# Windowed attention: the value projection in four pieces, one a round, with earlier output transposes and transposes of 113 rows

## The chip, the cores and the metric

The kernel runs on one core of one Trainium2 chip. The metric is the device time of one execution, in microseconds (us), the median of the runs of one kernel. A change of about 2% is what separates faster or slower from no change here.

## The reference, cut to what matters

`x` is (16, 64, 56, 56) in float32. Two attention layers follow each other, each on a group-normalised input and each with a residual. The change touches the first alone:

```python
t = xn.reshape(Bb, Cc, WS, n1, WS, n2).transpose(0, 3, 5, 2, 4, 1)
tok = t.reshape(Bb * n1 * n2, WS * WS, Cc)          # windows of 49 tokens
qk = (tok @ qk_w.T).reshape(-1, WS * WS, 2, HEADS, DH)
attn = softmax(einsum('bhqd,bhkd->bhqk', q, k) * scale)
v = relu(tok @ v_w.T)
o = einsum('bhqk,bhkd->bhqd', attn, v)
x = x + out                                          # residual
```

The reshapes take four windows together: 196 tokens of 64 channels become 49 rows of 16 heads of 16, so a softmax runs over 49 keys, for 256 groups of four windows. The second layer is a 5x5 local attention with a softmax over 25 neighbours; the change does not touch it.

## The kernel before, in words

Two images lie side by side on the 128 partitions (2 x 64 channels), 8 such pairs. A **unit** is one row of 8 windows (two groups of four) in both images of a pair, 392 columns on 128 partitions; there are 64 units. Units 0 to 6 are written out (PEEL), units 7 to 62 run in a loop of two units a turn, and unit 63 is written out again. Units 0 to 5 also carry the statistics of the later images on VectorE, and unit 6 turns them into scales.

Each unit has four **rounds**, k = 0 to 3. A round handles one image's group of four windows, with its 16 heads; its number over the whole stage is n = 4u + k. The steps are software-pipelined over rounds and units, and each engine runs its list in the order in which it is written; semaphores tie the lists together. In round k of unit u:

- TensorE: `scores(n)` into PSUM banks 2 and 3; `transpose_probs(n-1)` (four transposes into bank 7); `weigh_values(n-2)` (into bank 6); in rounds 1 and 2 one half of `project_qk` for unit u+1; then a wait until VectorE has taken this round's scores out of banks 2 and 3 (`sub_done`) and GpSimd has expanded the next keys (`kbd_ready`); then `transpose_v` in round 0, one half of `project_v` (bank 0, for unit u+1) in rounds 1 and 2, `transpose_output` of unit u-1 in round 3. `transpose_v` and `transpose_output` share bank 1.
- VectorE: `subtract_max(n)` (the maximum, then the subtraction), `normalise(n-2)`, and in round 3 `order_tokens(u-1)`, two copies out of bank 1 that put the result in token order; in round 1 the statistics of a finished unit.
- ScalarE: `copy_transposed(n-1)` out of bank 7, `exponentials(n)`, then `place_values` in rounds 0 and 1, `copy_qk` for unit u+1 in rounds 2 and 3, `gather(u+2)` in round 2 and `copy_v(u+1)` last in round 3. `copy_v` counts `proj_copied` up to 3(u+2).
- GpSimd: `expand_keys` for each round, and `add_residual(u-2)` in round 1. SyncE stores the finished units.

`await_project(u+1)` in TensorE's list waits for the tokens of unit u+1 and for `proj_copied` at 3(u+1), that is for `copy_v(u)`: banks 0, 4 and 5 are written again after it. It stands in round 1 before `transpose_probs`. `transpose_v(u)` waits for the same count. Each attention matrix has 49 real rows in a slot of 64, two slots in 128 rows: rows 113 to 127 are padding. The lines of the profile: `scores` L1312, `transpose_probs` L1321, `weigh_values` L1337, `project_qk` L1281, `project_v` L1289, `transpose_v` L1300, `transpose_output` L1351; VectorE L1100, L1104 (`subtract_max`), L1114, L1117 (`normalise`), L1129 (`order_tokens`); ScalarE L844 (`gather`), L850 (`copy_qk`), L854 (`copy_v`), L863 (`place_values`), L868 (`exponentials`), L875 (`copy_transposed`).

Of the kernel before, what the change touches and what calls it, by code (L numbers as in the profile page):

```python
# [21 lines left out]
P = 128  # L22
# [8 lines left out]
S = WS * WS  # L31
SP = 64
ELT = 4 * S
UT = 2 * ELT
HEADS_R = 8
HEADS_T = HEADS_R // 2
UNITS = BP * NI
# [7 lines left out]
STATS_UNIT = 6  # L45
# [255 lines left out]
def build(nc, x, bn_gamma, bn_beta, bn_mean, bn_var, qk_w, v_w, w_out, b_out, out):  # L301
# [11 lines left out]
    with ExitStack() as ctx:  # L313
# [20 lines left out]
        ident = const(P)  # L334
# [370 lines left out]
        def _(pool):  # L705
# [38 lines left out]
            for u in range(2):  # L744
                for b2 in range(2):
                    nc.gpsimd.memset(qk_sb[u][b2][:, UT:UT + SP], 0.0)
                    nc.gpsimd.memset(v_bd[u][b2], 0.0)
                nc.gpsimd.memset(v_ch[u], 0.0)
            nc.gpsimd.memset(zeros, 0.0).then_inc(zeros_ready, 1)
            for q in probs:  # L750
                i = nc.gpsimd.memset(q, 0.0)
# [76 lines left out]
        def _(act):  # L828
# [42 lines left out]
            def copy_transposed(n, k, ready=True):  # L871
                act.wait_ge(pt_done, n + 1)
                if not (isinstance(n, int) and n < 2):
                    act.wait_ge(pv_done, n - 1)
                nc.scalar.activation(probs_T[k % 2].rearrange("p j n -> p (j n)"), PS[:, 7, :],  # L875
                                     ACT.Copy).then_inc(pt_copied, 1)

            gather(0, 0)
# [146 lines left out]
        def _(dve):  # L1025
# [70 lines left out]
            def subtract_max(n, k):  # L1096
                b0, b1 = score_banks
                bank = PS[:, b0:b1 + 1, 0:HEADS_T * SP].rearrange("p i (j s) -> p i j s", s=SP)[:, :, :, 0:S]
                dve.wait_ge(s_done, n + 1)
                nc.vector.tensor_reduce(by_tile(row_max[k % 2]), bank, AX_X, ALU.max).then_inc(max_done, 1)  # L1100
                dve.wait_ge(max_done, n + 1)
                if not (isinstance(n, int) and n < 4):
                    dve.wait_ge(pt_done, n - 3)
                nc.vector.tensor_tensor(probs[k].rearrange("p (j i) s -> p i j s", i=2)[:, :, :, 0:S], bank,  # L1104
                                        by_tile(row_max[k % 2]).unsqueeze(3).to_broadcast([P, 2, HEADS_T, S]),
                                        ALU.subtract).then_inc(sub_done, 1)
# [24 lines left out]
            def unit(u, up, first, last):  # L1131
                for k in range(4):
                    n = 4 * u + k
                    subtract_max(n, k)
                    if not (first and k < 2):
                        normalise(n - 2, (k - 2) % 4, up if k >= 2 else 1 - up)
                    if isinstance(u, int) and u == STATS_UNIT and k >= 1:
                        i = group_stats(k - 1, 1, CHUNKS)
                        if k == 3:
                            affine(group_stats(3, 1, CHUNKS), PAIRS_OF_TURN[1])  # L1140
                    if k == 3 and not first:
                        order_tokens(u - 1, 1 - up)
                    if k == 1 and not (isinstance(u, int) and u < 4):
                        unit_stats(u - 4)
                    if isinstance(u, int) and u < STATS_UNIT:
                        step(stats(STATS_OF[n]))
# [105 lines left out]
        def _(pe):  # L1252
# [6 lines left out]
            def pair_means(turn, k):  # L1259

                pe.wait_ge(gn_in, 2 * turn + k + 1)
                nc.tensor.matmul(PS[:, 1, 0:BP], pair_mean, t_tmp, start=True, stop=True).then_inc(gn_out, 1)
# [20 lines left out]
                if h == 1:  # L1283
                    i.then_inc(qk_done, 1)

            def project_v(up, h):

                cols = slice(h * ELT, (h + 1) * ELT)
                i = nc.tensor.matmul(PS[:, 0, cols], wv_T, tok[up][:, cols], start=True, stop=True)  # L1289
                if h == 1:  # L1290
                    i.then_inc(v_done, 1)

            def transpose_v(u, up):
# [22 lines left out]
            def transpose_probs(n, k):  # L1316
                pe.wait_ge(exp_done, n + 1)
                if not (isinstance(n, int) and n < 1):
                    pe.wait_ge(pt_copied, n)
                for j in range(4):  # L1320
                    i = nc.tensor.transpose(PS[:, 7, j * P:(j + 1) * P],  # L1321
                                            probs[k][:, 2 * j:2 * j + 2, :].rearrange("p h s -> p (h s)"), ident)
                i.then_inc(pt_done, 1)

            def await_values(n, vbd):
# [15 lines left out]
            def await_output(u):  # L1341

                pe.wait_ge(norm_done, 4 * u + 4)
                pe.wait_ge(vbd_ready, 2 * UNITS if isinstance(u, int) and u == UNITS - 1 else 2 * u + 4)

            def transpose_output(up):

                for e in range(2):
                    for h in range(2):
                        q = 2 * e + h  # L1350
                        i = nc.tensor.transpose(PS[:, 1, q * P:(q + 1) * P], o_tok[up][:, e, h].rearrange("p b c -> p (b c)"), ident)  # L1351
                i.then_inc(ot_done, 1)

            await_project(0)
            for h in range(2):
                project_qk(0, h)
                project_v(0, h)

            def unit(u, up, first, last):
                for k in range(4):  # L1360
                    n = 4 * u + k
                    m = (k - 2) % 4
                    scores(n, k, up)
                    if not (first and k < 2):
                        await_values(n - 2, 2 * u + m % 2 + 1 - (0 if k >= 2 else 2))
                    if k == 1 and not last:
                        await_project(u + 1)
                    if not (first and k == 0):
                        transpose_probs(n - 1, (k - 1) % 4)
                    if not (first and k < 2):  # L1370
                        weigh_values(n - 2, m, up if k >= 2 else 1 - up)
                    if k in (1, 2) and not last:
                        project_qk(1 - up, k - 1)
                    if isinstance(u, int) and u == STATS_UNIT and k >= 2:
                        pe.wait_ge(vbd_ready, 2 * u + 2)
                        pair_means(1, k - 2)
                        if k == 3:
                            pe.wait_ge(sq_in, 2)
                    if k == 3 and not first:
                        await_output(u - 1)  # L1380
                    if not (last and k == 3):
                        pe.wait_ge(kbd_ready, n + 2)
                        pe.wait_ge(sub_done, n + 1)
                    if k == 0:
                        transpose_v(u, up)
                    elif k in (1, 2) and not last:
                        project_v(1 - up, k - 1)
                    elif k == 3 and not first:
                        transpose_output(1 - up)
            units(pe, unit, peel=PEEL)  # L1390
            transpose_probs(4 * UNITS - 1, 3)
            for k in (2, 3):
# [127 lines left out]
```

## Time and profile before

| what | value |
|---|---|
| median of 3 runs | 1789.05 us (1788.67 to 1808.39) |
| the profiled execution | 1798.7 us, span 1797.0 us |
| first attention | until about 770 us of the span |
| VectorE's share of the span | 80% |
| TensorE's share of the span | 80% |

The profile is of one execution. A row of its timeline gives the start and length of a group of equal instructions, both in us; TensorE matmuls are pipelined, so one's length reaches into the next, and what a step costs is read from its start to the start of the next step. "PEld" is the load of the stationary operand. A float32 matmul is listed as two instructions, a transpose as one. The value in brackets is the idle time ahead of the row and the instruction that ended it.

### The profile page before, as it was taken

The numbers are of one execution on the slowest core, as the hardware profiler recorded it, in microseconds if no ns is written. First come the engines' busy times: TensorE is split into PE (matmuls) and PEld (weight loads), VectorE is DVE, ScalarE is ACT, GpSimd is POOL, SyncE is SP. The second block draws the span as 40 slices with busy tenths as digits, with TensorE's granted clock in tenths as the row PEclk, the third lists the DMA queues.
The fourth block names the chain that finished last, engine by engine and source line by source line (L and its number), as shares of the span: only waits on it lengthen the run. The fifth ranks groups of instructions, "written<-read, shape, count | busy, mean of one in ns | idle before, by whom it ended". The sixth has DMA issues, their size and how long they took to land.

```text
span 1797.0 us, 60281 instructions
## 1 busy us (share of the span) xinstructions
PE 1435.7 (80%) x25001; PEld 704.2 (39%) x25001; DVE 1434.3 (80%) x1975; ACT 1051.5 (59%) x1883; POOL 1187.3 (66%) x860
## 2 busy tenths in 40 slices
PE   4999999999999999936887869777786876867745
PEld 2656666666666666610222212212221221213322
DVE  4776777777777777769999998999989899995924
ACT  3446777777777777735555747466574656543300
POOL 5334555555555555500999899999999999995700
PEclk9568999999999999956898998999999899997868
DMA  8702010202015101060225133252312422026079
GB/s 334 278 11 55 18 54 18 54 18 54 18 49 87 54 18 54 18 165 7 56 51 128 29 75 78 50 129 51 88 49 59 115 51 67 22 68 247 21 289 390
DMA packets 106860, 156.12 MB, mean 87 GB/s; under 512 B 71362, under 2 KB 83650, under 8 KB 100034
## 3 DMA queue, kind: packets, MB, share of 16 engines
q1 hardware_dynamic: 106690, 153.60, 29.2%
q8 instruction: 137, 2.24, 0.5%
q14 instruction: 33, 0.27, 0.1%
HBM read 81.92 MB, written 65.20 MB: 82 GB/s over the span
## 4 chain that ended last, share of the span: by engine, by line
PE 39%; POOL 27%; DVE 16%; issue 12%; ACT 2%; SPq 1%; DMA 1%; DVEq 0%; POOLq 0%
POOL arena L800 20%; PE PS L1312 6%; PE PS L1471 5%; PE PS L1321 5%; PE PS L1337 5%; POOL arena L811 4%; DVE arena L1104 4%; PE PS L1289 4%; DVE arena L1100 4%; PE PS L1281 4%; PE PS L1494 3%; PE PS L1300 2%; PE PS L1351 2%; DVE arena L1211 2%; PE PS L1419 2%
## 5 line engine op out<-in xcount | busy, mean ns | idle before, releaser
L800 POOL TENSOR_TENSOR arena<-arena 128x2016 f32<-128x2016 f32 (+2 forms) x168 | 604.9, 3635 | 78.9 <-PE PS L1419 78.7
L1211 DVE TENSOR_TENSOR arena<-arena,PS 128x1568 f32<-128x1568 f32 x348 | 610.3, 1778 | 39.6 <-PE PS L1471 32.6
L766 POOL TENSOR_TENSOR arena<-arena,consts 128x196 f32<-128x196 f32 x512 | 294.3, 608 | 278.1 <-ACT arena L850 278.1
L1471 PE MATMUL PS<-arena,consts 32*32 32x392 f32 x12800 | 391.3, 513 | 83.8 <-DVE arena L1211 46.9
L992 ACT ACTIVATE PS<-arena 128x392 f32<-128x392 f32 x348 | 172.9, 499 | 271.4 <-DVE arena L1211 269.5
L1419 PE MATMUL PS<-arena,consts 128*32 128x504 f32 (+2 forms) x1664 | 225.6, 618 | 119.9 <-POOL arena L800 76.7
L1471 PEld LDWEIGHTS PS<-arena,consts 32*32 32x32 f32 x12800 | 140.2, 104 | 337.4 <-DVE arena L1211 179.1
L1100 DVE TENSOR_REDUCE arena<-PS 128x8 f32<-128x392 f32 x256 | 143.3, 560 | 142.3 <-PE PS L1312 140.9
L875 ACT ACTIVATE arena<-PS 128x512 f32<-128x512 f32 x256 | 153.0, 598 | 155.0 <-PE PS L1321 151.6
L811 POOL TENSOR_TENSOR arena<-arena 128x1568 f32<-128x1568 f32 x52 | 159.3, 3076 | 49.0 <-ACT arena L938 21.6
L1321 PE MATMUL PS<-consts,arena 128*128 128x128 f32 x1024 | 176.6, 297 | 0.2
L1337 PE MATMUL PS<-arena 128*64 128x34 f32 x4096 | 175.8, 231 | 0.7 <-DVE arena L1117 0.7
L1312 PE MATMUL PS<-arena 64*64 64x196 f32 x2048 | 165.9, 396 | 1.9 <-POOL arena L766 1.1
L1337 PEld LDWEIGHTS PS<-arena 128*64 128x64 f32 x4096 | 146.6, 143 | 46.5 <-issue 45.7
L1104 DVE TENSOR_TENSOR arena<-PS,arena 128x392 f32<-128x392 f32 x256 | 145.5, 568 | 18.7
L868 ACT ACTIVATE arena<-arena 128x392 f32<-128x392 f32 x256 | 137.8, 538 | 33.1 <-DVE arena L1104 24.1
L773 POOL TENSOR_TENSOR arena<-arena 128x392 f32 (+1 forms) x64 | 78.5, 1226 | 108.8 <-DVE arena L1129 108.8
L1419 PEld LDWEIGHTS PS<-arena,consts 128*32 128x32 f32 x1664 | 37.2, 112 | 282.4 <-POOL arena L800 97.1
L1321 PEld LDWEIGHTS PS<-consts,arena 128*128 128x128 f32 x1024 | 113.0, 146 | 63.9 <-issue 51.3
L929 ACT ACTIVATE arena<-arena,consts 128x616 f32<-128x616 f32 x128 | 111.8, 907 | 5.3 <-DVE consts L1171 4.6
L863 ACT ACTIVATE arena<-PS 49x256 f32<-49x256 f32 x256 | 95.7, 374 | 24.3 <-PE PS L1300 22.8
L1312 PEld LDWEIGHTS PS<-arena 64*64 64x64 f32 x2048 | 84.1, 200 | 56.5 <-issue 54.8
(105 smaller groups left out, 1670.6 us busy)
## 6 DMA issues: line engine op xcount, KB each, us to landing
arena<-x_wide_dram SPq DMA_DIRECT2D x256, 82.5 KB, 2.1
arena<-x_wide_dram SPq DMA_DIRECT2D x32, 660.0 KB, 8.3
x_wide_dram<-arena SPq DMA_DIRECT2D x12, 1125.0 KB
arena<-in_x_dram SPq DMA_DIRECT2D x8, 1568.0 KB, 15.2
x_wide_dram<-arena SPq DMA_DIRECT2D x64, 196.0 KB, 4.4
x_dram<-arena SPq DMA_DIRECT2D x8, 1568.0 KB, 7.4
attn_dram<-arena SPq DMA_DIRECT2D x256, 49.0 KB, 2.9
arena<-x_dram SPq DMA_DIRECT2D x8, 1568.0 KB, 18.9
```

What stands on the lines that cost most here:

```text
L766: i = nc.gpsimd.tensor_tensor(k_bd[k][:, r], keys.unsqueeze(1).to_broadcast([P, HEADS_T, S]), head_mask.unsqueeze(2).to_broadcast([P, HEAD ...
L800: nc.gpsimd.tensor_tensor(tile, x_part, by, ALU.mult).then_inc(pool_tile, 1)
L811: nc.gpsimd.tensor_tensor(tile, *by, ALU.mult).then_inc(pool_tile, 1)
L992: nc.scalar.activation(PS[:, 2 + n % W_BANKS, 0:PIX], sc[j % 2][:, k, :], ACT.Copy).then_inc(weight_placed, 1)
L1100: nc.vector.tensor_reduce(by_tile(row_max[k % 2]), bank, AX_X, ALU.max).then_inc(max_done, 1)
L1104: nc.vector.tensor_tensor(probs[k].rearrange("p (j i) s -> p i j s", i=2)[:, :, :, 0:S], bank, by_tile(row_max[k % 2]).unsqueeze(3).to_bro ...
L1211: nc.vector.tensor_tensor(by_channel(v_tiles[n % V_RING]), shifted_values(half, k), over_channels(PS[:, 2 + n % W_BANKS, 0:PIX]), ALU.mult ...
L1312: mm = nc.tensor.matmul(dst, residue(qk_sb[up][b2], e, r)[rows], k_bd[k][rows, r], start=True, stop=True)
L1321: i = nc.tensor.transpose(PS[:, 7, j * P:(j + 1) * P], probs[k][:, 2 * j:2 * j + 2, :].rearrange("p h s -> p (h s)"), ident)
L1337: i = nc.tensor.matmul(PS[rows, 6, VW * j:VW * j + VN], probs_T[k % 2][:, j, rows], v_bd[up][e][:, b2 * 4 + j + 8 * r, 0:VN], start=True, ...
L1419: mm = nc.tensor.matmul(PS[g * GROUP:(g + 1) * GROUP, 0, 0:rows * cols], fold, tile[:, g * rows * cols:(g + 1) * rows * cols], start=a == ...
L1471: mm = nc.tensor.matmul(PS[dst, 4 + i, 0:PIX], ident[src, src], tile[src, c * PIX:(c + 1) * PIX], start=done == 0, stop=done == NK - 1)
```

## The change

- `project_v` is cut from two halves of 196 columns into four pieces of 98, one in every round, after the wait for `sub_done` and `kbd_ready`.
- `await_project(u+1)` moves from round 1 to round 0, still ahead of `transpose_probs`.
- `transpose_output` moves from the end of round 3 to right behind its scores, ahead of `transpose_probs`; `order_tokens` on VectorE moves ahead of `normalise` in round 3.
- `transpose_v` stands ahead of the wait in round 0 instead of behind it.
- `transpose_probs` and `transpose_output` take 113 rows in place of 128, so each writes 113 columns; `copy_transposed` copies 4 x 113 columns in place of 512, and GpSimd fills both `probs_T` with 1.0 once at the start.

```diff
+            for t in probs_T:
+                nc.gpsimd.memset(t, 1.0)
...
-                nc.scalar.activation(probs_T[k % 2].rearrange("p j n -> p (j n)"), PS[:, 7, :],
+                nc.scalar.activation(probs_T[k % 2][:, :, 0:PAIR], PS[:, 7, :].rearrange("p (j n) -> p j n", j=4)[:, :, 0:PAIR],
...
                     subtract_max(n, k)
+                    if k == 3 and not first:
+                        order_tokens(u - 1, 1 - up)
                     if not (first and k < 2):
                         normalise(n - 2, (k - 2) % 4, up if k >= 2 else 1 - up)
...
-                    if k == 3 and not first:
-                        order_tokens(u - 1, 1 - up)
...
-                cols = slice(h * ELT, (h + 1) * ELT)
+                cols = slice(piece * UT // 4, (piece + 1) * UT // 4)
                 i = nc.tensor.matmul(PS[:, 0, cols], wv_T, tok[up][:, cols], start=True, stop=True)
-                if h == 1:
+                if piece == 3:
                     i.then_inc(v_done, 1)
...
-                    i = nc.tensor.transpose(PS[:, 7, j * P:(j + 1) * P],
-                                            probs[k][:, 2 * j:2 * j + 2, :].rearrange("p h s -> p (h s)"), ident)
+                    i = nc.tensor.transpose(PS[:, 7, j * P:j * P + PAIR],
+                                            probs[k][0:PAIR, 2 * j:2 * j + 2, :].rearrange("p h s -> p (h s)"), ident[0:PAIR, 0:PAIR])
...
                     scores(n, k, up)
+                    if k == 3 and not first:
+                        await_output(u - 1)
+                        if isinstance(u, int) and u == STATS_UNIT:
+                            pe.wait_ge(gn_in, 4)
+                        transpose_output(1 - up)
                     if not (first and k < 2):
                         await_values(n - 2, 2 * u + m % 2 + 1 - (0 if k >= 2 else 2))
-                    if k == 1 and not last:
+                    if k == 0 and not last:
                         await_project(u + 1)
...
-                        if k == 3:
+                    if k == 0:
+                        if isinstance(u, int) and u == STATS_UNIT + 1:
                             pe.wait_ge(sq_in, 2)
-                    if k == 3 and not first:
-                        await_output(u - 1)
+                        transpose_v(u, up)
                     if not (last and k == 3):
                         pe.wait_ge(kbd_ready, n + 2)
                         pe.wait_ge(sub_done, n + 1)
-                    if k == 0:
-                        transpose_v(u, up)
-                    elif k in (1, 2) and not last:
-                        project_v(1 - up, k - 1)
-                    elif k == 3 and not first:
-                        transpose_output(1 - up)
+                    if not last:
+                        project_v(1 - up, k)
```

TensorE's list, rounds 0 and 1 of a unit in the loop, before; L1312 are the scores that open a round, and L1272 belongs to `await_project`:

```order
L1312 MATMUL PS<-arena 64x4x49 x4
L1327 ISA
L1328 ISA
L1330 REGISTER_ALU
L1321 MATMUL PS<-consts,arena 128x128 x4
L1337 MATMUL PS<-arena 64x34 x8
L1382 REGISTER_ALU
L1383 REGISTER_ALU
L1295 ISA
L1297 REGISTER_ALU
L1300 MATMUL PS<-consts,arena 128x128 x4
L1312 MATMUL PS<-arena 64x4x49 x4
```

The same place in the changed kernel, whose line numbers lie 3 or more higher (L1315 are the scores, L1275 belongs to `await_project`, L1292 is the value projection):

```order
L1315 MATMUL PS<-arena 64x4x49 x4
L1330 ISA
L1331 ISA
L1333 REGISTER_ALU
L1273 REGISTER_ALU
L1275 ISA
L1324 MATMUL PS<-consts,arena 128x113 x4
L1340 MATMUL PS<-arena 64x34 x8
L1298 ISA
L1300 REGISTER_ALU
L1303 MATMUL PS<-consts,arena 128x128 x4
L1393 REGISTER_ALU
```

The wait of `await_project` now comes before round 0's transposes, and L1393, the wait for VectorE and GpSimd, behind the transposes of the values instead of ahead of them.

VectorE's list in round 3 before, from the maximum (L1100) to the two ordering copies (L1129):

```order
L1100 TENSOR_REDUCE arena<-PS 128x2x4
L1104 TENSOR_TENSOR arena<-PS,arena 128x2x4x49
L1114 RECIPROCAL arena<-PS 128x8
L1117 TENSOR_TENSOR arena<-PS,arena 128x4x2x16
L1125 REGISTER_ALU
L1129 COPY arena<-PS 128x2x2x49 x2
```

And in the changed kernel, where the copies are L1132:

```order
L1103 TENSOR_REDUCE arena<-PS 128x2x4
L1107 TENSOR_TENSOR arena<-PS,arena 128x2x4x49
L1128 REGISTER_ALU
L1132 COPY arena<-PS 128x2x2x49 x2
L1117 RECIPROCAL arena<-PS 128x8
L1120 TENSOR_TENSOR arena<-PS,arena 128x4x2x16
```

The normalisation now stands behind the copies.

## Rows read from the trace of the kernel before

**Rows 1.** The page: TensorE's busy time, and its granted clock in 40 slices.

```profile
PE 1435.7 (80%) x25001; PEld 704.2 (39%) x25001; DVE 1434.3 (80%) x1975; ACT 1051.5 (59%) x1883; POOL 1187.3 (66%) x860
PEclk9568999999999999956898998999999899997868
```

**Rows 2.** Busy time of each engine in four stretches of the first attention.

```profile
core 0: us, PE busy (x) PEld busy (x) DVE busy (x) ACT busy (x) POOL busy (x), PEclk, DMA share, GB/s
152.12:757.40 605.28, 563.33 (x7701) 386.54 (x7702) 430.86 (x1046) 451.08 (x880) 317.62 (x496) 1.00 0.17 41
...
49.99:53.40 3.41, 1.96 (x35) 1.43 (x28) 3.31 (x9) 1.35 (x3) 2.42 (x4) 1.00 1.01 420
...
53.40:104.60 51.20, 50.73 (x411) 31.75 (x412) 33.76 (x76) 22.87 (x47) 15.81 (x25) 0.50 0.48 176
118.26:145.56 27.30, 26.15 (x198) 16.46 (x198) 16.00 (x46) 13.47 (x26) 7.21 (x12) 0.50 0.08 16
```

**Rows 3.** Timeline of TensorE over one unit, from a round 3 on.

```profile
301.30 0.62 PE L1312 MATMUL PS<-arena 64*64 64x196 f32 x8
...
303.30 0.63 PE L1351 MATMUL PS<-consts,arena 128*128 128x128 f32 x4 [0.21 <-DVE arena L1104]
303.86 0.62 PE L1312 MATMUL PS<-arena 64*64 64x196 f32 x8
...
306.22 0.65 PE L1300 MATMUL PS<-consts,arena 128*128 128x128 f32 x4 [0.55 <-DVE arena L1104]
306.80 0.62 PE L1312 MATMUL PS<-arena 64*64 64x196 f32 x8
307.35 0.66 PE L1321 MATMUL PS<-consts,arena 128*128 128x128 f32 x4
307.94 0.66 PE L1337 MATMUL PS<-arena 128*64 128x34 f32 x16
308.53 0.56 PE L1281 MATMUL PS<-arena,consts 64*64 64x196 f32 x8
309.02 0.60 PE L1289 MATMUL PS<-arena,consts 128*128 128x196 f32 x2
309.55 0.62 PE L1312 MATMUL PS<-arena 64*64 64x196 f32 x8
```

**Rows 4.** Single instructions of a value projection and of four transposes, by narrow windows.

```profile
309.13 0.19 PEld L1289 LDWEIGHTS PS<-arena,consts 128*128 128x128 f32 x1
309.29 0.33 PE L1289 MATMUL PS<-arena,consts 128*128 128x196 f32 x1
310.10 0.14 PEld L1321 LDWEIGHTS PS<-consts,arena 128*128 128x128 f32 x1 [0.22 <-ACT arena L863]
310.16 0.14 PEld L1321 LDWEIGHTS PS<-consts,arena 128*128 128x128 f32 x1
310.38 0.38 PE L1321 MATMUL PS<-consts,arena 128*128 128x128 f32 x2
310.49 0.27 PE L1321 MATMUL PS<-consts,arena 128*128 128x128 f32 x1
```

**Rows 5.** Timeline of ScalarE and VectorE in the same round 3.

```profile
301.37 1.11 ACT L844 ACTIVATE arena<-arena,consts 128x392 f32 x1
...
302.54 0.60 ACT L875 ACTIVATE arena<-PS 128x512 f32<-128x512 f32 x1
...
303.19 0.54 ACT L868 ACTIVATE arena<-arena 128x392 f32<-128x392 f32 x1
...
303.38 0.29 DVE L1117 TENSOR_TENSOR arena<-PS,arena 128x128 f32<-128x128 f32 x1
303.63 0.48 ACT L850 ACTIVATE arena<-PS 128x392 f32<-128x392 f32 x1
...
304.01 0.50 ACT L854 ACTIVATE arena<-PS 128x392 f32<-128x392 f32 x1
304.06 0.86 DVE L1129 COPY arena<-PS 128x196 f32<-128x196 f32 x2 [0.38 <-PE PS L1351]
```

More of the change, by code:

```diff
@@ L34 @@
 UT = 2 * ELT
+PAIR = SP + S
 HEADS_R = 8
@@ L1284, in project_qk, with project_v @@
                     i.then_inc(qk_done, 1)
-            def project_v(up, h):
-                cols = slice(h * ELT, (h + 1) * ELT)
+            def project_v(up, piece):
+                cols = slice(piece * UT // 4, (piece + 1) * UT // 4)
                 i = nc.tensor.matmul(PS[:, 0, cols], wv_T, tok[up][:, cols], start=True, stop=True)
-                if h == 1:
+                if piece == 3:
                     i.then_inc(v_done, 1)
@@ L1350, in transpose_output @@
                         q = 2 * e + h
-                        i = nc.tensor.transpose(PS[:, 1, q * P:(q + 1) * P], o_tok[up][:, e, h].rearrange("p b c -> p (b c)"), ident)
+                        i = nc.tensor.transpose(PS[:, 1, q * P:q * P + PAIR], o_tok[up][0:PAIR, e, h].rearrange("p b c -> p (b c)"), ident[0:PAIR, 0:PAIR])
                 i.then_inc(ot_done, 1)
@@ L1356, in _ @@
                 project_qk(0, h)
-                project_v(0, h)
+            for piece in range(4):
+                project_v(0, piece)
             def unit(u, up, first, last):
@@ L1375, in unit @@
                         pe.wait_ge(vbd_ready, 2 * u + 2)
+                        if k == 3:
+                            pe.wait_ge(res_ready, 2 * u)
                         pair_means(1, k - 2)
-                        if k == 3:
+                    if k == 0:
+                        if isinstance(u, int) and u == STATS_UNIT + 1:
                             pe.wait_ge(sq_in, 2)
-                    if k == 3 and not first:
-                        await_output(u - 1)
+                        transpose_v(u, up)
                     if not (last and k == 3):
```

## The prediction

> **What bounds the kernel now.** I read the page first. Both TensorE and VectorE are busy for 80% of the span [rows 1], an average over stages with different limits, so I went to the first attention alone, the only stage that the change touches; the second layer behind it keeps its instructions. Next, the table of stretches. From 152.12 to 757.40 us, 55 units at 605.28/55 = 11.005 us, TensorE is busy for 93%, ScalarE for 75% and VectorE for 71%, at the full clock [rows 2]: TensorE's list is the bound there. Two stretches ahead of that ran at half the clock, 51.2 and 27.3 us [rows 2], so at 1.2 in place of 2.4 GHz.
>
> Then the timeline of one unit. Taken from scores to scores, round 3 is 303.86 - 301.30 = 2.56 us, round 0 is 306.80 - 303.86 = 2.94, round 1 is 2.75 [rows 3], and round 2 is what is left of 11.005, 2.75 as well. Only two rows have an idle time ahead of them: 0.21 before the output transposes of round 3 and 0.55 before the value transposes of round 0, both until VectorE's subtraction has read the score banks [rows 3]. Rounds 1 and 2 have none; they are full of TensorE's own steps. By their starts [rows 3] the steps cost: scores 0.55, transposes of probabilities 0.59, weighing 0.59, half a query/key projection 0.49, half a value projection 0.53, and 0.56 to 0.58 for the output and value transposes.
>
> Last, single instructions. Transposes follow each other by 310.49 - 310.38 = 0.11 us, and their first load takes 310.16 - 310.10 = 0.06 [rows 4]; what is left of the 0.59, 0.09 us, is the gap at the change from one tile shape to the next. In the value projection the first load takes 309.13 - 309.02 = 0.11 and the first matmul 309.29 - 309.13 = 0.16 for 196 columns; the second takes as much, and 0.10 pass until the next step's load [rows 3, 4].
>
> **The change part by part, per unit at the full clock.**
>
> *Quarters of the value projection.* A piece has 98 columns, so its two matmuls stream for 0.08 each. It still loads its stationary operand twice, 0.11 each. The second load runs beside the first matmul but is longer than it: 0.11 + 0.11 + 0.08 + 0.09 = 0.39 against 0.53. No row shows a piece of 98 columns. The bounds are 0.53 (nothing saved) and 0.53/2 = 0.27 (all of it in proportion). I take 0.39, because both loads are visible in rows 4. Rounds 1 and 2 lose 0.14 each; rounds 0 and 3 gain 0.39 each.
>
> *113 columns.* If the columns set the 0.11, 15 of 128 fewer save 0.013 per transpose, 0.05 for four. The bounds are 0 and 0.05. I take 0.05, because the second load began 0.06 behind the first, so a load is shorter than the pitch [rows 4]. A group of four is then 0.54.
> The Trainium skill, "TensorE: Matmul & The Clock Gate", section LDWEIGHTS, says that a load takes its columns over 1.2 GHz, whatever the rows. By that, an estimate, the 128 stationary columns, which the change keeps, need 0.107 us and set the pitch alone, and narrower transposes would save nothing; the 0.06 here speaks against it for transposes, while the 0.11 of the value projection agrees.
>
> *Rounds 1 and 2.* 0.55 + 0.54 + 0.59 + 0.49 + 0.39 = 2.56 each. The wait now precedes the last 0.39. VectorE's result comes 303.30 - 301.30 = 2.00 behind the start of the scores [rows 3], while TensorE arrives at 2.17: no wait.
>
> *Round 3.* The output transposes follow the scores and run into the probability transposes with the same shape, so one gap and one load fall away: 0.55 + 0.06 + 8 x 0.097 + 0.09 = 1.48, with the weighing 2.07, just past VectorE's 2.00, and with a piece 2.46.
>
> *Round 0, where a new wait comes.* `await_project` now stands ahead of this round's transposes and needs `copy_v`, ScalarE's last step of the round 3 before. I follow that chain from the start of round 3. The eight transposes last until 0.55 + 0.61 + 4 x 0.097 = 1.55. The copy out of bank 7 starts 0.04 later, at 1.59 (the gather before it would let it start at about the same time: 302.54 behind a gather that ends at 302.48 [rows 5]). Neighbouring ScalarE steps overlap by 0.10 (304.01 against 303.63 + 0.48 [rows 5]). The copy of 452 columns takes 0.55, so the exponential starts at 2.04. Then come 0.44 to `copy_qk` and 0.38 to `copy_v`, which starts at 2.86 and ends at 3.36; with 0.13 for the signal (as from the subtraction's end at 303.17 to TensorE at 303.30), TensorE may go on at 3.49. Round 3 ended at 2.46, so this is 1.03 into round 0, where TensorE is ready at 0.55. **A wait of 0.48 us appears on ScalarE**, behind which the transposes, the weighing and the scores of round 1 queue on TensorE. A second gate lies behind it: the normalisation, which ended at 303.67, 2.37 into round 3, now comes after ordering copies of 0.86, so it ends at 3.23 at the latest and with its signal would hold TensorE until 0.90 [rows 3, 5].
> The rest of round 0: 0.54, 0.59, and then value transposes (0.06 + 4 x 0.11 = 0.50) and a piece. Whether the gap of 0.09 and the exposed load of 0.11 stand between those two no row shows, for transpose and matmul of one shape never follow each other in this stage. Bounds: 0.20 and 0. I take 0, since every gap that the rows show lies at a change of shape. The round is 1.03 + 0.54 + 0.59 + 0.50 + 0.28 = 2.94. Bounds 2.94 and 3.14. VectorE's 2.00 is over by then: the old wait of 0.55 is gone and 0.48 is back.
>
> *Off the path.* The two memsets cost GpSimd about 1 us at the start, under waits of other engines for the weights; if that cover were gone, 1 us. The residual can start earlier, and the stores with it, with nobody waiting. `order_tokens` loses its wait of 0.38 [rows 5] on an engine that is not the bound.
>
> *Sum.* 2.46 + 2.94 + 2.56 + 2.56 = 10.52 against 11.005: 0.485 per unit, over the 56 units from the eighth on 27 us. In units 0 to 6 I forecast no gain: part of them runs at half the clock, and VectorE with its statistics sets the pace of the others. Against the profiled execution that is 1798.7 - 27 = 1772. That execution lies 9.65 above the median of the runs shown, so the same difference on 1789.05 gives **1762 us**, 1.5% less.
>
> **Rivals.**
>
> *The early clock holds, or the wait is smaller.* The first low stretch begins behind a window in which TensorE was busy for only 1.96 of 3.41 us while VectorE was busy for 3.31 [rows 2]: VectorE was late, in a round 3 whose ordering copies waited for transposes that now come early, and behind TensorE's wait stands one step more to do first. Matmuls per us tell the low clock's price: a unit has 7701/55 = 140, so the low stretches hold 411/140 = 2.9 and 198/140 = 1.4 units [rows 2], which at the full clock take 32 and 16 us: 19 and 12 us lost. Without the first the time is 1743, without both 1731. If `copy_v` comes early as well, the normalisation's gate decides and 0.13 x 56 = 7 us more go. For it: less idle time on VectorE. Against: its statistics alone keep it full there. Chance 0.33.
>
> *The load sets the transposes' pitch.* Then 0.05 comes back in each of the four groups of probabilities and in the output group: 0.25 x 56 = 14 us, 1776. Chance 0.12. The rule of the Trainium skill above would have it so.
>
> *The pieces cost 0.53 and the gap stays before round 0's piece.* 4 x 0.14 + 0.2 = 0.76 per unit, so 11.28: 15 us slower than before, 1804. Against: 98 columns have to stream faster than 196. Chance 0.07.
>
> *Slower: the clock falls in the loop.* The wait of round 0 and the long run of transposes in round 3 lie in one stretch, and TensorE's clock drops as it did at 53.40. A low unit costs 51.2/2.9 - 11 = 6.7 us more. It decides the other way once it holds for ten units (27 gained and 36 lost need 63 us), 1829. Against: the idle time per unit falls from 0.76 to 0.48, and the clock stood through all 55 units [rows 2]. Chance 0.06.
> The Trainium skill, "TensorE: Matmul & The Clock Gate", section PE-mode transpose, says that transposes do not count as busy for the clock gate; the change lets eight stand together, but makes fewer columns of them.
>
> The forecast has 0.42. Range: it must reach down to 1732 and up to 1796, which leaves out parts of the two ends. A measurement of this kernel tells about 2% (36 us, so 1753 and 1825) from no change: faster 0.35, within 0.58, slower 0.07.
>
> **What would show it.** After: a row of `project_v` with 98 columns and 0.39 to the next scores; rounds 1 and 2 at 2.56; in round 3 output and probability transposes back to back; in round 0 an idle time before the probability transposes of about 0.5 ended by ScalarE's `copy_v`, and none before the value transposes; a unit of 10.5. I am wrong if the idle time in round 0 names VectorE or is missing, if transposes keep their 0.11, or if the granted clock has other low stretches than before 150 us.

## The result, and the profile after

| | before | changed |
|---|---|---|
| median | 1796.56 us (4 runs) | 1752.9 us (4 runs) |
| runs | 1788.67, 1789.05, 1804.07, 1808.39 | 1731.47, 1733.84, 1771.96, 1901.34 |
| ratio | 1 | 0.9639, 95% interval 0.9525 to 0.9753 |
| profiled execution | 1798.7 | 1733.84 |

The comparison leaves out executions far above the fastest of the same kernel, so the ratio speaks for the two near 1732; the experiments show that the higher ones belong to this kernel. I had forecast 1762, 27 us less; between the two profiled executions it is 65.

The granted clock of the page and the busy shares by stretch, of the changed kernel:

```profile
PEclk9999999999999999766999989999999899998978
```

```profile
134.80:697.90 563.10, 547.27 (x7781) 403.75 (x7780) 416.72 (x1028) 414.37 (x865) 312.64 (x487) 1.00 0.18 44
25.40:110.70 85.30, 71.62 (x980) 51.08 (x972) 77.89 (x188) 56.35 (x115) 41.91 (x67) 1.00 0.70 249
110.70:117.60 6.90, 5.11 (x38) 3.85 (x38) 2.55 (x8) 3.26 (x6) 0.16 (x1) 0.51 0.01 2
```

Slices 1 to 16 of the page read 9, where [rows 1] had 5, 6 and 8 in the second to fourth. TensorE is now busy for 547.27/563.10 = 97% of the loop, against 93% [rows 2]. The two low stretches of 51.2 and 27.3 us [rows 2] have become one of 6.9. The timeline of TensorE over one unit, to be laid beside [rows 3]:

```profile
301.65 0.62 PE L1315 MATMUL PS<-arena 64*64 64x196 f32 x8
302.56 0.61 PE L1324 MATMUL PS<-consts,arena 113*128 113x113 f32 x4 [0.28 <-ACT arena L857]
303.09 0.66 PE L1340 MATMUL PS<-arena 128*64 128x34 f32 x16
303.68 0.65 PE L1303 MATMUL PS<-consts,arena 128*128 128x128 f32 x4
304.18 0.36 PE L1292 MATMUL PS<-arena,consts 128*128 128x98 f32 x2
304.47 0.62 PE L1315 MATMUL PS<-arena 64*64 64x196 f32 x8
305.02 0.60 PE L1324 MATMUL PS<-consts,arena 113*128 113x113 f32 x4
305.56 0.66 PE L1340 MATMUL PS<-arena 128*64 128x34 f32 x16
306.15 0.56 PE L1284 MATMUL PS<-arena,consts 64*64 64x196 f32 x8
306.64 0.47 PE L1292 MATMUL PS<-arena,consts 128*128 128x98 f32 x2
307.03 0.62 PE L1315 MATMUL PS<-arena 64*64 64x196 f32 x8
...
309.60 0.62 PE L1315 MATMUL PS<-arena 64*64 64x196 f32 x8
310.15 0.61 PE L1354 MATMUL PS<-consts,arena 113*128 113x113 f32 x4
310.60 0.55 PE L1324 MATMUL PS<-consts,arena 113*128 113x113 f32 x4
311.07 0.66 PE L1340 MATMUL PS<-arena 128*64 128x34 f32 x16
311.67 0.46 PE L1292 MATMUL PS<-arena,consts 128*128 128x98 f32 x2
312.06 0.62 PE L1315 MATMUL PS<-arena 64*64 64x196 f32 x8
```

From scores to scores, rounds 0 to 3 take 2.82, 2.56, 2.57 and 2.46 us, the unit 312.06 - 301.65 = 10.41. The only idle time is that of round 0, ended by `copy_v` (L857). ScalarE in the round 3 before that, beside [rows 5]:

```profile
300.75 0.55 ACT L878 ACTIVATE arena<-PS 128x452 f32<-128x452 f32 x1 [0.16 <-PE PS L1324]
301.20 0.53 ACT L871 ACTIVATE arena<-arena 128x392 f32<-128x392 f32 x1
301.62 0.49 ACT L853 ACTIVATE arena<-PS 128x392 f32<-128x392 f32 x1
302.00 0.51 ACT L857 ACTIVATE arena<-PS 128x392 f32<-128x392 f32 x1
```

`copy_v` ends at 302.51, 0.86 into round 0, and the transposes start at 302.56, 0.91 into it. Over the 55 units from unit 8 to unit 63 a unit takes 10.43 on average.

Where the 65 us went is read from the scores that open units 8 and 63. Before:

```profile
149.76 0.62 PE L1312 MATMUL PS<-arena 64*64 64x196 f32 x8
...
755.20 0.46 PE L1312 MATMUL PS<-arena 64*64 64x196 f32 x4
```

After:

```profile
124.13 0.46 PE L1315 MATMUL PS<-arena 64*64 64x196 f32 x4
...
697.86 0.62 PE L1315 MATMUL PS<-arena 64*64 64x196 f32 x8
```

Unit 8 opens 149.76 - 124.13 = 25.6 us earlier. The 55 units up to unit 63 take 573.73 in place of 605.44 us, 31.7 less. The rest, which the change does not touch, is 1732.1 - 697.86 = 1034.2 in place of 1797.0 - 755.20 = 1041.8, 7.6 less. That part is not a gain of the change: another execution of the same changed kernel (`a0_after` below) takes 1041.7 for it.

The 25.6 us are the clock's. Units 2, 3 and 4 took 17.24, 17.69 and 17.69 us before and 11.53, 11.51 and 12.33 after, unit 6 took 19.53 and then 13.64. In the profile of before, the clock fell at 53.40 behind an idle time of 1.45 us in round 0 of unit 2, and at 118.26 in one of 1.99 us in round 0 of unit 6:

```profile
52.80 0.63 PE L1300 MATMUL PS<-consts,arena 128*128 128x128 f32 x4 [1.45 <-issue]
```

In the changed kernel the longest idle time in units 1 to 6 is 0.88 us, and the clock holds. It falls in unit 7, at 110.7, inside a wait of 4.14 us for the tokens that ScalarE gathers (L847) behind its two table loads, at the place to which `await_project` was moved:

```profile
112.49 0.99 PE L1324 MATMUL PS<-consts,arena 113*128 113x113 f32 x4 [4.14 <-ACT arena L847]
```

### The profile page after: what moved, and what is told of

It reads as the page before. It is cut to its first block, busy times and chain, and to the rows that moved or that the text cites. A ratio compares the mean times of both kernels' runs of the same rounds, so it can differ in the third digit from the quotient of the medians.

```text
span 1732.1 us, 60795 instructions
## 1 busy us (share of the span) xinstructions
PE 1390.4 (80%) x25257; PEld 712.2 (41%) x25257; DVE 1424.8 (82%) x1975; ACT 1020.4 (59%) x1883; POOL 1188.8 (69%) x862
## 4 chain that ended last, share of the span: by engine, by line
PE 40%; POOL 28%; issue 12%; DVE 10%; ACT 6%; SPq 1%; DMA 1%; POOLq 0%; ACTq 0%; DVEq 0%
POOL arena L803 21%; PE PS L1324 7%; PE PS L1340 6%; PE PS L1315 6%; POOL arena L814 5%; PE PS L1478 5%; PE PS L1292 3%; PE PS L1284 3%; PE PS L1501 3%; DVE arena L1214 2%; PE PS L1426 2%; POOL arena L819 2%; PE PS L1303 2%; DVE arena L1187 2%; PE PS L1354 2%
## 5 line engine op out<-in xcount | busy, mean ns | idle before, releaser
L1214 DVE TENSOR_TENSOR arena<-arena,PS 128x1568 f32<-128x1568 f32 x348 | 609.5, 1777 | 37.0 <-PE PS L1478 30.6
L1478 PE MATMUL PS<-arena,consts 32*32 32x392 f32 x12800 | 387.3, 507 | 83.5 <-DVE arena L1214 47.9
L878 ACT ACTIVATE arena<-PS 128x452 f32<-128x452 f32 x256 | 141.3, 552 | 142.2 <-PE PS L1324 141.4
L1324 PE MATMUL PS<-consts,arena 113*128 113x113 f32 x1024 | 152.1, 271 | 24.5 <-ACT arena L857 19.7
L1340 PE MATMUL PS<-arena 128*64 128x34 f32 x4096 | 169.5, 227 | 0.7 <-DVE arena L1120 0.7
L1315 PE MATMUL PS<-arena 64*64 64x196 f32 x2048 | 160.0, 383 | 0.7 <-DVE arena L1107 0.7
L1340 PEld LDWEIGHTS PS<-arena 128*64 128x64 f32 x4096 | 140.6, 138 | 37.1 <-ACT arena L878 0.8
L1324 PEld LDWEIGHTS PS<-consts,arena 113*128 113x128 f32 x1024 | 104.0, 142 | 72.3 <-issue 39.1
L1292 PE MATMUL PS<-arena,consts 128*128 128x98 f32 x512 | 112.5, 303 | 6.5 <-DVE arena L1107 5.6
L969 ACT ACTIVATE arena<-PS 128x392 f32<-128x392 f32 x104 | 51.0, 491 | 93.9 <-PE PS L1426 93.9
L1197 DVE TENSOR_TENSOR PS<-arena,PS 128x392 f32<-128x392 f32 x184 | 102.4, 556 | 2.2
```

The lines of the kernel that those rows point to most:

```text
L1214: nc.vector.tensor_tensor(by_channel(v_tiles[n % V_RING]), shifted_values(half, k), over_channels(PS[:, 2 + n % W_BANKS, 0:PIX]), ALU.mult ...
L1315: mm = nc.tensor.matmul(dst, residue(qk_sb[up][b2], e, r)[rows], k_bd[k][rows, r], start=True, stop=True)
L1324: i = nc.tensor.transpose(PS[:, 7, j * P:j * P + PAIR], probs[k][0:PAIR, 2 * j:2 * j + 2, :].rearrange("p h s -> p (h s)"), ident[0:PAIR, ...
L1340: i = nc.tensor.matmul(PS[rows, 6, VW * j:VW * j + VN], probs_T[k % 2][:, j, rows], v_bd[up][e][:, b2 * 4 + j + 8 * r, 0:VN], start=True, ...
L1478: mm = nc.tensor.matmul(PS[dst, 4 + i, 0:PIX], ident[src, src], tile[src, c * PIX:(c + 1) * PIX], start=done == 0, stop=done == NK - 1)
```

## The experiments

Theory A: the loop gains what its steps say, and all else is the clock of the first 150 us and how long it stays low. Rival B: the low stretches are chance, and they neither depend on the kernel nor set its spread. What A says of the clock changed on the way. In the first set it was that the change keeps the early clock full, so that the changed kernel would not spread; from the second set on it was that the pattern of a low unit decides how long the clock stays low.

All executions of each kernel, in us. A unit at 2.4 GHz is the average of the full-clock units from unit 8 on; "up to" marks a low stretch that began ahead of unit 0.

| kernel | executions | unit at 2.4 GHz | low unit | low before unit 63, profiled run |
|---|---|---|---|---|
| before | 1773 to 1814 over all sets | 11.01 | 17.7 | 51, 27 |
| changed, 12 runs in 3 sets | 1731, 1734, 1737, 1759, 1760, 1772, 1818, 1831, 1846, 1888, 1901, 1901 | 10.43 | 17.2 | 7; up to 465; up to 98, and 14 |
| b_filled | 1772 to 1788 (10) | 11.01 | 18.3 | up to 61, and 14 |
| qn_no_moves | 1781, 1789, 1790, 1794, 1798, 1876, 1884, 1886, 1887, 1892, 1980 | 10.81 | 17.1 | 17, 334 |
| a_await_late | 1757, 1776, 1777, 1803 | 10.11 | 17.2 | 143 |
| qm_128_rows | 1755, 1757, 1763, 1776 | 10.73 | 17.7 | up to 64, and 44 |
| n_113_rows | 1814, 1826, 1836, 1836 | 10.86 | 16.9 to 17.3 | 10, 215 |
| a_filler | 1731, 1756, 1761, 1761, 1770, 1804 | 10.43 | 17.7 | up to 99, and 14 |
| late_filler, 10 runs in 2 sets | 1733, 1734, 1736, 1738, 1739, 1741, 1745, 1745, 1767, 1779 | 10.33 | 17.75 | up to 64, and 3; 20 |
| n_113_filler | 1779, 1780, 1789, 1796, 1799, 1805, 1806, 1818, 1818 | 10.85 | 17.45 | 20, 72 |
| late_fill_r2 | 1744, 1754, 1787, 1820 | 10.37 | 17.75 | 41 |

The median of the twelve executions of the changed kernel is 1795, the same as that of the kernel before (1792 to 1797 over its sets). The 3.6% of the table above hold for the executions in which the low stretches stay short.

**a0_after and a0_again: the changed kernel, unedited.**

> The changed kernel again, unedited, to see how its time and its clock's low stretches spread. Theory A (the loop's shorter unit gives about 33 us, and the full clock in units 0 to 6 gives the other 25 to 31): unit of 10.41 us in the loop, no low stretch of more than about 7 us before unit 8, fast runs 1730 to 1740. Rival B (the early clock was luck of that execution): low stretches of 27 or 51 us come back before 150 us in this profile, and fast runs spread up to 1765.

> The changed kernel again beside late_filler_2 on one chip. Theory A: unit of 10.41 us at the full clock, 17.2 at the low one, and runs anywhere from 1731 to 1900 by the unit in which the clock rises (6.8 us for each low unit: 0 to 25 low units). Rival B: near 1735 here, the two slow sets having been of their chips.

The first set's profile is of the execution of 1900.77 us, and units 8 to 24 were 17.21 us long each. The value transposes (L1303) around the turn, 17.21 and then 12.03 us apart:

```profile
443.85 1.12 PE L1303 MATMUL PS<-consts,arena 128*128 128x128 f32 x4
...
461.06 1.12 PE L1303 MATMUL PS<-consts,arena 128*128 128x128 f32 x4
...
473.09 0.66 PE L1303 MATMUL PS<-consts,arena 128*128 128x128 f32 x4
```

Four transposes fall from 1.12 to 0.66 us; behind the turn the unit is 10.43. (In this execution the granted clock is not recorded ahead of the turn; the durations are those of the half clock in the kernels below, where it is.) The scores of unit 0 are already at the half clock (0.94 us in place of 0.62), so here the clock did not fall: it had not yet risen. Against the profile of the first table unit 8 opens at 165.67 in place of 124.13, 41.5 us later, and the 55 units take 691.37 in place of 573.73, 117.6 more; with 7.5 in the second layer that is the whole difference of 166.7 between the two spans. A low unit in the loop costs 17.21 - 10.43 = 6.8 us more.

Both theories were right on the loop. On the clock both missed in the first set: A expected 1730 to 1740, met by one execution in four, and B at most 1765. The second set, beside `late_filler_2`, ran from 1759 to 1846, which is the spread that A by then expected and not the 1735 of B; in its profile the clock rose at 97.8 and unit 8 opened at 148.52.

**b_filled: before, with the idle time of round 0 filled in units 1 to 6.**

```diff
-                        weigh_values(n - 2, m, up if k >= 2 else 1 - up)
+                        weigh_values(n - 2, m, up if k >= 2 else 1 - up,
+                                     2 if isinstance(u, int) and 0 < u <= STATS_UNIT and k == 0 else 1)
```

The last argument is the number of times that the eight products are made.

> The kernel before, with weigh_values of round 0 done twice in units 1 to 6 (the same results written again, 0.59 us more of matmuls inside the idle time ahead of the value transposes). Theory A (TensorE's idle time in these rounds lets the clock fall, and the clock costs the time): the clock stays at 2.4 GHz from 53 to 105 us, unit 8 starts about 19 us earlier (31 if the second stretch goes too), the loop keeps 11.005 per unit, time 1758 to 1775. Rival B (the clock falls for another reason, the full DMA load or VectorE's own lateness): the stretches stay and the time is that of before, or some us more.

Ratio 0.9929 (0.9893 to 0.9964), median 1781.7 against 1793.15: less than the 2% that counts as faster, but clear of noise. The clock was full from 61 to 125.8 us:

```profile
61.00:125.80 64.80, 54.91 (x801) 38.61 (x800) 57.70 (x145) 42.45 (x83) 28.42 (x45) 1.00 0.30 98
125.80:139.50 13.70, 12.40 (x92) 7.33 (x92) 6.32 (x15) 6.68 (x13) 5.49 (x9) 0.50 0.09 16
```

More work made the kernel 11 us faster, in the direction of A, but less than the 19 expected. The two low parts that remain, up to 61 us and the one that begins in an idle time of 2.78 us behind the table loads of unit 7, were not hit.

**qn_no_moves: the changed kernel with the bank-1 steps in their old places.**

```diff
-                        await_output(u - 1)
...
-                        transpose_output(1 - up)
...
+                    if k == 0:
+                        transpose_v(u, up)
+                    elif k == 3 and not first:
+                        transpose_output(1 - up)
                     if not last:
                         project_v(1 - up, k)
```

`order_tokens` goes back behind `normalise` as well.

> The changed kernel with the output transposes, the value transposes and order_tokens back in their old places (behind the wait; behind normalise), quarters and 113 rows kept. Theory A: round 3's VectorE waits for the transposes again, so the early clock falls as before (low stretches of 27 us or more before 150 us), and in the loop rounds 0 and 3 have the transposes behind the wait for the subtraction: round 3 = 2.00 + 0.54 + 0.39 = 2.93 or so, round 0 3.2, unit 11.2, time 1790 to 1815. Rival (the quarters alone give the gain): unit 10.5, time about 1735 to 1765.

The unit was 10.81, not 11.2: I had put a change of tile shape between the transposes and the piece behind them, and there is none. So these three moves are worth 0.38 us per unit, and what is left in place (quarters, narrow transposes, the moved `await_project`) is worth 0.20 together. The waits that the moves remove:

```profile
506.29 0.58 PE L1354 MATMUL PS<-consts,arena 113*128 113x113 f32 x4 [0.26 <-DVE arena L1107]
...
509.18 0.65 PE L1303 MATMUL PS<-consts,arena 128*128 128x128 f32 x4 [0.31 <-DVE arena L1107]
```

Six of eleven executions took 1876 us or more; the profiled one was low for 334.5 us:

```profile
79.60:414.10 334.50, 329.96 (x2767) 226.42 (x2767) 170.35 (x397) 151.49 (x311) 110.31 (x174) 0.50 0.10 22
```

**n_113_rows: before, with 113-row transposes alone.**

```diff
-                    i = nc.tensor.transpose(PS[:, 7, j * P:(j + 1) * P],
-                                            probs[k][:, 2 * j:2 * j + 2, :].rearrange("p h s -> p (h s)"), ident)
+                    i = nc.tensor.transpose(PS[:, 7, j * P:j * P + PAIR],
+                                            probs[k][0:PAIR, 2 * j:2 * j + 2, :].rearrange("p h s -> p (h s)"), ident[0:PAIR, 0:PAIR])
```

The output transposes, the copy (now 452 columns) and the two memsets are edited as in the change.

> The kernel before with 113-row transposes alone. In the loop: rounds 1 and 2 of 2.75 lose 0.05 each, rounds 0 and 3 wait for VectorE anyway and lose nothing or 0.05: unit 10.85 to 10.91 (the rule that the load sets the pitch: 11.005). Theory A on the clock: a low unit gets shorter than 17.7 us (about 17.2 to 17.3), and low stretches of over 100 us appear in some runs, so that runs spread from 1775 to over 1830. Rival B: the spread stays that of before, 1782 to 1814, some us lower.

The unit fell to 10.86 as expected (the rule that the load sets the pitch would have left it at 11.005), yet the kernel was slower than before, ratio 1.0167 (1.0105 to 1.0229). The reason stands in the clock's column:

```profile
42.10:257.20 215.10, 211.72 (x1740) 133.95 (x1740) 124.35 (x293) 97.60 (x202) 69.45 (x109) 0.50 0.24 81
257.20:793.40 536.20, 493.36 (x6919) 341.00 (x6918) 379.89 (x938) 393.54 (x790) 285.30 (x445) 1.00 0.18 41
```

This is the cleanest evidence against B: an edit that only shortens steps made every one of four executions slower than all 11 of before beside them (1784 to 1804).

**qm_128_rows: the changed kernel with 128-row transposes.** The diff is the reverse of the one above, in both places.

> The changed kernel with 128-row transposes and the full 512-column copy again; the quarters and the moves kept. In the loop at the full clock, both theories: 20 transposes take 0.11 in place of 0.097, so a unit of 10.41 + 0.2 to 0.25 = 10.6 to 10.65. On the clock: theory A (what decides the time of the changed kernel is how long the clock stays at 1.2 GHz once it is there, and that hangs on the pattern of a low unit, 17.2 us there against 17.7 before): a low unit is again about 17.7 us, low stretches end within some 60 us as in the kernel before, and all runs lie within 1735 to 1775. Rival B (the falls are chance of the early idle time and their length is chance too): low stretches of over 100 us appear, runs spread up to 1850 and more.

The unit was 10.73 (10.6 to 10.65 expected), so narrow transposes, with the shorter copy behind them, save 0.30 per unit. Yet the four executions lie within 1755 to 1776, ratio 0.9793 (0.9744 to 0.9842). The profiled one was low up to 64 us and once more for 44. A, as expected: slower steps, and a lower median than that of the changed kernel.

**a_await_late: `await_project` behind `weigh_values`.**

```diff
-                    if k == 0 and not last:
-                        await_project(u + 1)
...
                         weigh_values(n - 2, m, up if k >= 2 else 1 - up)
+                    if k == 0 and not last:
+                        await_project(u + 1)
```

> The changed kernel with await_project in round 0 behind weigh_values instead of ahead of transpose_probs. Theory A (copy_v on ScalarE is the gate of the 0.30 to 0.36 us of idle time in round 0): the idle time goes or falls to under 0.1, where the normalisation is the next gate; round 0 2.50 to 2.55, unit 10.1, 17 us less than the changed kernel, about 1715. Rival (the gate is the transposes' own input or the normalisation, which end at about the same time): unit stays at 10.35 to 10.41.

Round 0 as predicted, 311.82 - 309.32 = 2.50 us, with the transposes 0.59 behind the scores:

```profile
309.32 0.62 PE L1315 MATMUL PS<-arena 64*64 64x196 f32 x8
309.91 0.61 PE L1324 MATMUL PS<-consts,arena 113*128 113x113 f32 x4
...
311.82 0.46 PE L1315 MATMUL PS<-arena 64*64 64x196 f32 x4
```

The unit is 10.11 in place of 10.43. That shows `copy_v` as the gate, which the row at 302.56 above names as well. The time missed the 1715: 143.3 us were low.

```profile
99.10:242.40 143.30, 140.72 (x1176) 96.73 (x1174) 70.35 (x171) 65.44 (x134) 45.82 (x72) 0.50 0.09 23
```

**a_filler and late_filler: one more matmul in round 0.** `late_filler` has the edit of `a_await_late` as well.

```diff
+                    if k == 0 and not first:
+                        pe.wait_ge(pt_copied, n - 1)
+                        nc.tensor.matmul(PS[:, 7, 0:128], wv_T, tok[up][:, 0:128], start=True, stop=True)
                     if not (first and k < 2):
                         await_values(n - 2, 2 * u + m % 2 + 1 - (0 if k >= 2 else 2))
```

> The changed kernel with one more matmul of 128 columns (into bank 7, overwritten behind it; it adds nothing to the result) in round 0 of every unit, between the scores and the transposes, where TensorE waits for copy_v. At the full clock it takes about 0.32 us of the 0.36 us of idle time, so the unit stays at 10.41 to 10.45. At the low clock it takes 0.64 us more: a low unit of 17.85 in place of 17.2 us. Theory A (the pattern of the low unit holds the clock down, and idle time lets it fall): low stretches end within some 60 us, runs 1730 to 1765, none over 1800. Rival B (chance): runs spread up to 1850 and 1900 as those of the changed kernel do.

> The same filler together with await_project behind weigh_values. The wait for copy_v is gone, so the filler is on the path: unit 10.06 + 0.32 = 10.4 at the full clock, about 17.85 at the low one. Theory A: like the run above, 1730 to 1765 with no long low stretch. Rival B: spread as in the changed kernel.

> late_filler again, unedited, in more rounds: both theories give a unit of 10.33 us in the loop; theory A: no run over 1770, median about 1740; rival B: single runs at 1800 to 1900 as in the changed kernel.

In `a_filler` the filler (L1375) fills the idle time, 307.81 - 307.45 = 0.36:

```profile
306.90 0.62 PE L1315 MATMUL PS<-arena 64*64 64x196 f32 x8
307.45 0.49 PE L1375 MATMUL PS<-arena,consts 128*128 128x128 f32 x2
307.81 0.32 PE L1324 MATMUL PS<-consts,arena 113*128 113x113 f32 x1
```

Ratio 0.971 (0.9632 to 0.9789) with one execution of six at 1804, which A had excluded. `late_filler` gave 0.9684 (0.962 to 0.9747) and, in more rounds, 0.9698 (0.9658 to 0.9738). Its ten executions lie within 1733 to 1779, median 1740, two of them over the 1765 or 1770 that I had named. Beside it on the same chip the changed kernel took 1759, 1760, 1831 and 1846. So this version, with useless work in it, is the best of all: its fastest equals the changed kernel's, and over all executions the medians are 1740 against 1795. Against `a_await_late`, from which it differs by the filler alone, they are 1740 and 1777.

**n_113_filler: the slower kernel, with a filler.** As above, in front of the wait of round 0, into bank 1.

```diff
+                    if k == 0 and not (isinstance(u, int) and u < 2):
+                        pe.wait_ge(res_ready, 2 * u - 2)
+                        nc.tensor.matmul(PS[:, 1, 0:128], wv_T, tok[up][:, 0:128], start=True, stop=True)
```

> The kernel before with 113-row transposes, as n_113_rows, and one filling matmul of 128 columns (into bank 1, overwritten by the value transposes behind it) in round 0 of every unit from 2 on, in the idle time ahead of the value transposes. At the full clock it fits into the 0.55 us of idle time: unit 10.86 as in n_113_rows. At the low clock a unit goes from 16.9 to about 17.5 us. Theory A (the pattern of the low unit holds the clock down): low stretches of under 100 us, time 1775 to 1795, so 35 to 50 us faster than n_113_rows (1814 to 1836) with more work to do. Rival B (chance, or 113 rows hurt in another way): 1815 to 1835 again.

Median 1799 against 1831, so 32 us faster than without it (in another set, on another chip; the kernel before took 1795 and 1796 beside them), with the same unit of 10.85. Against before the ratio is 0.9985 (0.9938 to 1.0032), no change. But six of nine executions were above the 1795 that I had set as the upper end, so half confirmed.

```profile
110.20:181.90 71.70, 71.44 (x585) 46.37 (x584) 37.25 (x95) 33.83 (x68) 22.96 (x36) 0.50 0.13 35
```

**late_fill_r2: the filler in round 2.**

```diff
-                    if k == 0 and not first:
+                    if k == 2:
                         pe.wait_ge(pt_copied, n - 1)
-                        nc.tensor.matmul(PS[:, 7, 0:128], wv_T, tok[up][:, 0:128], start=True, stop=True)
+                        nc.tensor.matmul(PS[:, 7, 0:128], wv_T, tok[1 - up][:, 0:128], start=True, stop=True)
```

> late_filler with the filling matmul in round 2 of a unit in place of round 0; everything else the same, so a unit of 10.38 us at the full clock and about 17.85 at the low one. Theory A1 (a low unit's length decides how soon the clock rises, wherever the extra work lies): low stretches under 60 us before unit 8, runs 1732 to 1775, median about 1742. Theory A2 (what the extra work adds just ahead of the point 6.5 us into a unit, in rounds 0 and 1, decides): a filler in round 2 doesn't help, low stretches of over 100 us, runs up to 1800 and more.

1744, 1754, 1787 and 1820: between the two. The profiled low stretch of 41 us is what the first theory (length) expected; that two of four executions lie over its 1775, one at 1820, speaks for the second (place). The low unit is the same 17.75 us as in `late_filler`, but the spread is wider; four executions do not part the two, and where the filler stands may matter beside its length.

## Why the prediction was wrong

**The steps of the loop were right.** A piece: 0.39 forecast, 307.03 - 306.64 = 0.39 measured. Rounds 1 and 2: 2.56 forecast, 2.56 and 2.57 measured. Round 3: 2.46 and 2.46, the two groups of transposes back to back. Behind the value transposes a piece costs 304.47 - 304.18 = 0.29 (0.28): no gap and no exposed load between a transpose and a matmul of one shape. A group of narrow transposes takes 305.56 - 305.02 = 0.54 (0.54), and `n_113_rows` is 0.15 us per unit faster by them, so the load does not set their pitch. The rule of the Trainium skill ("TensorE: Matmul & The Clock Gate", LDWEIGHTS) would have left it at 0.59: here the measurement decides against it. The new wait behind `copy_v` is there and `a_await_late` shows its cause.

**One size was off there.** I let TensorE go on 0.13 us after `copy_v`, and it took 0.05; `copy_v` itself ended 0.86 into round 0, not 0.90. So round 0 is 2.82, not 2.94, the unit 10.43 on average, not 10.52, and the 55 units give 31.7 us instead of 26.7.

**The step that failed** is "In units 0 to 6 I forecast no gain". In the profiled execution unit 8 opened 25.6 us earlier, because neither of the two low stretches came, only one of 6.9 us. I had worked out that case and gave it 0.33 beside the forecast. Its price of 31 us was somewhat high: it takes 11 us for a unit at the full clock, and units 2 to 6 took 11.5 to 13.6.

The deeper fault is that I treated the low stretches as a thing of the kernel before that either stays or goes. In the three profiles of the changed kernel unit 8 opens at 124.13, 148.52 and 165.67, against 149.76 before: the 25.6 us belong to a lucky execution, and in another the forecast of no gain would have held. Of the six profiles with narrow transposes and no filler, four have a low stretch of 143, 215, 334 or some 440 us; in the other eight, with wide transposes or a filler or both, none reaches 100. So the change moves the time both ways, from 1731 to 1901. My slower rival had this price, a low unit 6.7 us dearer (6.8 measured), but put the fall in the loop, with 0.06. In no profile did the clock fall between units 8 and 63; it was already low when the loop began and stayed so. Half of twelve executions were over 1800.

**How sure this is.** Shown: the unit lengths, the price of a low unit, and that narrow transposes alone make the kernel slower through a long low stretch (`n_113_rows`). Supported by few executions each: that wide transposes (`qm_128_rows`) or a filler make it short again. Not simply so: the shorter the low unit, the longer the stretch, for 215 us came with 16.91 and 334 with 17.14.

Where the clock falls is seen well. In the profiled executions it fell 17 times between unit 0 and unit 8, each time in an idle time of TensorE of 0.87 us or more or at most 1.8 us behind its end. In 15 of the 17 this idle time began in round 0; in six it was that of unit 7, behind the table loads. Idle times of up to 0.57 us, one in every unit of the loop before, were followed by no fall. This gives no threshold: idle times of 0.86 to 0.88 in units 4 to 6 of the changed kernel were followed by none, one of 0.87 in `a_filler` was. It also shows why the moves help early on, together with `b_filled`; but one profile each does not show that they always keep the clock.

In six of the fourteen profiles the clock had been low since before unit 0 and rose for the first time in unit 2 or later, so their first low stretch is not a fall; why the clock rises so late there is open. It rose 16 times in units 1 and later (unit 7 left out), ten of them 6.47 to 6.67 us behind the scores that open a unit, in seven kernels. Open: why that point, and whether length or place of the added work is what helps. The second layer, which no edit touches, took 1032 to 1035 us in nine of the fourteen profiles and 1040 to 1042 in five, for the changed kernel as for others, so the 7.6 us say nothing on the change.

## What to carry to other kernels

Where the trace shows stretches at half the clock, ask of each edit what it does to the work inside them, and look at every execution, not at the lowest times: a shorter step can cost more than it saves if the low clock then lasts. A wait that an edit moves is priced well by following the late engine's list step by step from the rows of the trace. Here a useless matmul of 128 columns per unit was worth some 30 us.

## What the runs showed of the hardware that I had not expected

- TensorE can stay at the low clock for hundreds of us while it is busy for all but a per cent or two: 211.72 of 215.10 us in `n_113_rows`, 329.96 of 334.50 in `qn_no_moves`.
- A float32 matmul behind transposes of the same tile shape had neither the gap of 0.09 us nor the exposed load of 0.11 that stood at a change of shape: a piece cost 0.29 us there and 0.39 elsewhere.
- TensorE started 0.05 us after ScalarE's `copy_v` ended, against 0.13 after VectorE's subtraction in the output transposes before.
